# High and low f16 halves of the FFN's middle tiles: one 128x256 instruction a tile, or one of 128x512 for two tiles

## The reference, cut to what matters

```python
x = x + 0.5 * ffn(layernorm(x))          # first FFN
x = x + ssm(layernorm(x))                # state space layer, 16 states, a scan over 2048 tokens
x = x + 0.5 * ffn(layernorm(x))          # second FFN

def ffn(x):                              # x: 2048 tokens x 512
    x1 = x @ quantize(w1).T              # 512 -> 1408, weights -1, 0, 1
    x2 = x @ quantize(w2).T
    return (sigmoid(x1) * x2) @ quantize(w3).T   # 1408 -> 512
```

## Time and profile before

| what | value |
|---|---|
| median of 3 runs | 788.9 us (787.84 to 790.49) |
| span of the profiled execution | 788.1 us |
| mean granted TensorE clock | 0.942 |
| TensorE matmul busy | 644.3 us (82%), 4852 instructions |
| VectorE busy | 662.6 us (84%), 1053 instructions |
| POOL busy | 604.7 us (77%), 479 instructions |
| ScalarE busy | 530.6 us (67%), 1137 instructions |

### The profile page before, as it was taken

The page is one execution under the profiler, slowest core; times in us unless marked ns, Lnnn a source line. Parts: engine busy times, 40 slices in busy tenths (PEclk is TensorE's granted clock), DMA queues, the critical chain, the costliest instruction groups (busy, mean ns, idle before and its releaser), DMA issues.

```text
span 788.1 us, 13737 instructions
## 1 busy us (share of the span) xinstructions
PE 644.3 (82%) x4852; PEld 525.4 (67%) x4852; DVE 662.6 (84%) x1053; ACT 530.6 (67%) x1137; POOL 604.7 (77%) x479
## 2 busy tenths in 40 slices
PE   4697785579889988998899889988899887357878
PEld 3576663267668776886688767876787766245767
DVE  3872799689998999899989999899889987899721
ACT  5776665667686777766795779576867784556431
POOL 0081898589898998899889899799889978689512
PEclk9999998679999999999999999999999999578989
DMA  9500579668875897498668776788758875876000
GB/s 360 165 1 3 165 164 199 168 141 177 187 180 129 180 208 184 103 204 194 151 139 204 164 166 167 173 168 195 179 135 172 184 175 124 186 170 127 27 1 27
DMA packets 42437, 121.06 MB, mean 154 GB/s; under 512 B 5888, under 2 KB 14848, under 8 KB 42368
## 3 DMA queue, kind: packets, MB, share of 16 engines
q0 software_dynamic: 18864, 68.69, 45.9%
q1 hardware_dynamic: 23504, 51.49, 20.1%
HBM read 47.03 MB, written 4.46 MB: 65 GB/s over the span
## 4 chain that ended last, share of the span: by engine, by line
DVE 32%; PE 32%; issue 13%; ACT 13%; POOL 7%; DMA 2%; DVEq 1%; ACTq 0%; POOLq 0%
PE work L402 23%; DVE states L911 19%; PE stat L402 7%; DVE shared L922 7%; POOL hid_lo L1088 4%; ACT decay L727 3%; POOL shared L1104 2%; DMA shared<-shared 2%; DVE hid L881 2%; ACT L656 1%; PE decay L402 1%; ACT dt L715 1%; ACT q L745 1%; ACT L715 1%; ACT L659 1%
## 5 line engine op out<-in xcount | busy, mean ns | idle before, releaser
L402 PE MATMUL work<-x_hi,q 128*128 128x256 f16 x1408 | 328.0, 281 | 47.5 <-DVE hid L881 20.4
L1104 POOL TENSOR_TENSOR shared<-u,b_row 128x1024 f32<-128x1024 f32 x127 | 345.0, 2735 | 0.5
L402 PE MATMUL work<-x_lo,q 128*128 128x256 f16 x1408 | 326.9, 281 | 0.0
L911 DVE TENSOR_TENSOR_SCAN states<-decay,last_state,shared 128x256 f32<-128x256 f32 x448 | 303.7, 738 | 10.0 <-ACT decay L727 2.4
L727 ACT ACTIVATE decay<-dt,a_neg 128x256 f32<-128x256 f32 x512 | 220.2, 466 | 98.3 <-DVE states L911 97.5
L402 PEld LDWEIGHTS work<-x_hi,q 128*128 128x128 f16 x1408 | 142.3, 101 | 83.0 <-DVE hid L881 32.7
L1088 POOL TENSOR_TENSOR hid_lo<-hid,hid_hi 128x256 f16<-128x256 f32 x176 | 139.9, 1015 | 73.3 <-ACT hid_hi L690 73.1
L402 PE MATMUL work<-hid_hi,q 128*128 128x256 f16 x693 | 155.0, 274 | 14.8 <-POOL hid_lo L1088 7.8
L1117 POOL DMA_DIRECT2D shared<-shared x124 | 133.5, 1077 | 36.9 <-DVE shared L922 21.7
L922 DVE TENSOR_TENSOR shared<-states,c_row 128x1024 f32<-128x1024 f32 x128 | 155.5, 1215 | 5.8 <-issue 0.2
L402 PEld LDWEIGHTS work<-x_lo,q 128*128 128x128 f16 x1408 | 142.0, 101 | 21.8 <-issue 1.4
(11 more groups left out here) (102 smaller groups left out, 569.5 us busy)
## 6 DMA issues: line engine op xcount, KB each, us to landing
shared<-shared POOLq DMA_DIRECT2D x131, 512.0 KB, 6.2
b_row<-bc_dram SPq DMA_DIRECT2D x32, 512.0 KB, 5.1
c_row<-bc_dram SPq DMA_DIRECT2D x32, 512.0 KB, 5.2
x_in<-xT SPq DMA_DIRECT2D x8, 512.0 KB, 6.2
outT<-shared SPq DMA_DIRECT2D x7, 512.0 KB, 3.2
shared<-w1T SPq DMA_DIRECT2D x4, 704.0 KB, 7.3
shared<-w2T SPq DMA_DIRECT2D x4, 704.0 KB, 11.8
shared<-w3T SPq DMA_DIRECT2D x3, 768.0 KB, 13.5
```

The lines of the kernel that those rows point to most:

```text
L402: return nc.tensor.matmul(out, lhsT, rhs, start=start, stop=stop)
L911: nc.vector.tensor_tensor_scan(out=states[:, k, :], data0=decay[pair][:, k % 2, :], data1=dbx[:, g % DBX_RING, k, :], initial=state, op0=A ...
L1104: nc.gpsimd.tensor_tensor(dbx[:, g % DBX_RING, :, :], u[:, par, :, :], bcast(b_row[:, group % 2, n % ROWS, :]), ALU.mult).then_inc(dbx_don ...
```

## The change

ScalarE's hidden_hi and POOL's hidden_lo do nothing at the places of tiles 0, 2, 4, 6 and 8. At the places of tiles 1, 3, 5, 7 and 9 they make two tiles, (0, 1), (2, 3) and so on, with one instruction of 128x512, and add 2 to hi_done or lo_done. Tile 10 is made alone as before. The ring's two slots of a pair lie side by side in both kinds of pass. The wait for the down product of the pass before moves from tile 0's place to tile 1's. Nothing else is changed: the tables, VectorE's hidden, and TensorE's waits are the same.

```diff
             def hidden_hi(f, which, h):
-                unit = KH * f + h
-                act.wait_ge(hid_done, unit + 1)
-                if h == 0 and not (isinstance(f, int) and f == 0):
+                if h % 2 == 0 and h < KH - 1:
+                    return
+                lo, n = (h - 1, 2) if h % 2 else (h, 1)
+                act.wait_ge(hid_done, KH * f + h + 1)
+                if lo == 0 and not (isinstance(f, int) and f == 0):
                     act.wait_ge(down_done, 2 * f)
-                nc.scalar.activation(hid_hi[:, h, :], hid[:, hid_slot(which, h), :], ACT.Copy).then_inc(hi_done, 1)
+                at = hid_slot(which, lo)
+                nc.scalar.activation(hid_hi[:, lo:lo + n, :], hid[:, at:at + n, :], ACT.Copy).then_inc(hi_done, n)
...
             def hidden_lo(f, which, h):
-                unit = KH * f + h
-                pool.wait_ge(hi_done, unit + 1)
-                nc.gpsimd.tensor_tensor(hid_lo[:, h, :], hid[:, hid_slot(which, h), :], hid_hi[:, h, :], ALU.subtract).then_inc(lo_done, 1)
+                if h % 2 == 0 and h < KH - 1:
+                    return
+                lo, n = (h - 1, 2) if h % 2 else (h, 1)
+                pool.wait_ge(hi_done, KH * f + h + 1)
+                at = hid_slot(which, lo)
+                nc.gpsimd.tensor_tensor(hid_lo[:, lo:lo + n, :], hid[:, at:at + n, :], hid_hi[:, lo:lo + n, :],
+                                        ALU.subtract).then_inc(lo_done, n)
```

## The result

| what | before | after |
|---|---|---|
| median of 16 runs each, us | 790.36 (787.58 to 793.79) | 794.69 (793.57 to 797.37) |
| ratio of the times | | 1.0057, 95% interval 1.0043 to 1.0072 |
| span of the profiled execution, us | 788.1 | 792.4 |
| mean granted TensorE clock | 0.942 | 0.939 |

The changed kernel is slower by 0.57%, more than the 0.3% that a measurement can tell. The 16 runs of the kernel before that were made beside it lie 1.5 us above the three that the prediction started from, so its 793.2 us is 1.5 us under the median of after; its span, 792.4 us, is the measured one.

The account below looks back on a forecast made before the run. No engine alone bounds the kernel; POOL's low halves feed TensorE's down product, for which VectorE waits. Terms 2.7 - 0.1 + 0.9 + 0.8 = +4.3 us on 788.9 gave 793.2 us, range 789.7 to 796.3.

Parts of the forecast that it names:

- A pair on POOL: One 512-column low half on POOL takes 1.14 us; other estimates were 1.07, 1.27 and 1.53.
- Steady chunks: Second pass, chunks 1 to 5: TensorE's down product waits for tile 7 too, losing 0.54 us a chunk, +2.7 us in all.
- The residual's wait: VectorE's wait for TensorE at a steady chunk's second residual grows from 1.40 to about 1.9 us.
- ScalarE's relief: In the second pass it brings VectorE's tile 10 forward 0.1 to 0.3 us, worth nothing while VectorE waits for TensorE.
- POOL's row: In a steady chunk POOL's run of low halves ends 0.1 us later than before, counted from its DMA issue.
- Within 0.1 us of POOL's need: In a steady chunk ScalarE's high half of tiles 8 and 9 is done near 488.4, about when POOL needs it.
- Chunk 6: VectorE may stall 1 us and TensorE run 0.4 us later, covered by the 4.11 us wait: nothing, +1 us if uncovered.
- Last chunk: Steps 12 to 15: longer low halves delay TensorE's down product by 0.9 us without slack (0.5 to 1.2).
- First pass of all: Pairs run when quantising doesn't, so TensorE's tile 10 comes 0.8 us later (0.3 to 1.4).
- no change: Rival: slack the profile doesn't show absorbs the half-microsecond steps, 790.7 us; chance 0.24.
- dearer pairs: Rival: loss in the same place, with a POOL pair at 1.27 to 1.53 us, 796.2 to 800 us; chance 0.10.
- faster by POOL's relief: Rival: low halves on the chain shrink 10%, -3.2 us, 785.7 us, needing pairs of 0.90 us at most; chance 0.10.

Follow-up runs that it names:

- Run 1: Kernel after with high halves on ScalarE one tile at a time at their old places, pairs on POOL only: ratio 1.0034, span 792.4 us.
- run 4: Kernel before, nothing paired, with TensorE's second-pass down product waiting for eight tiles instead of seven: ratio 1.0022, span 792.5 us.
- run 6: The change's pairs only in the second FFN passes of the steady chunks, single instructions elsewhere: ratio 1.0041, span 793.3 us.
- run 3: Kernel after with TensorE's down product starting at six tiles instead of seven, waiting one by one from tile 6: ratio 1.0030, span 790.9 us.
- run 11: Kernel after, unchanged, profiled a second time: span 794.4 us.
- run 7: The change's pairs only in the very first pass and the last chunk's second pass, single instructions elsewhere: ratio 1.0021, span 789.3 us.
- run 5: The change's pairs only in the first FFN's passes except the very first, single instructions elsewhere: ratio 1.0010, span 789.5 us.
- run 9: Kernel before, no pairs, with tile 3's low half one place earlier on POOL, ahead of the DMA issue: ratio 0.9968, median 789.38 us.
- run 10: Kernel before, unchanged, profiled a second time: span 788.7 us.

## Why the prediction was right

It was right in sign, in size (ratio 1.0057 against 793.2 / 788.9 = 1.0055) and in the place. By its own steps:

- **A pair on POOL**: 1.14 us forecast, 1.137 measured. Taking it from the same operation at 1024 columns was the right choice: half of that, 1.07, the two single halves, 1.27, and the fold's 1.53 were all off.
- **Steady chunks**: +0.54 each forecast, +0.53 by the pitch. The down product is 0.67 us later behind the variance (0.7 forecast), and tile 10 no longer holds it. Run 1 shows that it is POOL's part, run 4 that the later gate alone is 0.31 of it, run 6 that it is these passes. The Trainium skill's Perfetto Trace Analysis, Optimizing Scalar/DVE Operations, was cited for two rules, which it gives for ScalarE and VectorE and which were applied to POOL here; the one on breaking instructions up where they cause bubbles elsewhere is what the trace bears out (TensorE's new wait of 0.41 us), though POOL's busy time fell by 14.8 us.
- **The residual's wait** was forecast at about 1.9 and is 2.16. The text had the reason, that ScalarE's relief ends in the same wait, and did not add it: tile 10's 0.25 us went there.
- **POOL's row** should have ended 0.1 us later; from the DMA issue's end it is 5.41 us (487.90 to 493.31) against 5.07, 0.34 later, by the 0.21 us that (8, 9) waits for ScalarE. "Within 0.1 us of POOL's need" was twice that. It cost nothing here, since tile 10's matmul stood at 493.64; in run 3 it took back part of the gain.
- **Chunk 6** was put at nothing and measured +0.36. The stall of VectorE for a ring slot came as described, 1.17 us at 658.22. It was hidden: VectorE waits at the residual behind it until TensorE is done, before and after (4.11 and 3.95 us). What was not hidden is TensorE's later run. The prediction counted the wait of 4.11 us as cover for it, but it is a wait for TensorE, so that the end of the down product sets it and a later end comes through. The 0.36 us that are left of the later start are that growth; the chunk's pitch is 84.46 or 84.47 in after and runs 6 and 11, and 84.10 and 84.11 in before and run 7.
- **Last chunk**: +0.9 forecast. TensorE's offset grows from 3.83 to 4.66, +0.83.
- **First pass of all**: +0.8 forecast, +0.54 measured. With chunk 6 this is the term that was mis-sized. The prediction kept pairs and quantising strictly apart and let each hold the other back. POOL and VectorE in time:

```profile
51.02 2.26 POOL L1094 TENSOR_TENSOR hid_lo<-hid,hid_hi 128x512 f16<-128x512 f32 x1 [0.37 <-ACT hid_hi L693]
53.46 3.08 POOL L1094 TENSOR_TENSOR hid_lo<-hid,hid_hi 128x512 f16<-128x512 f32 x2 [0.18 <-ACT hid_hi L693]
```

```profile
53.07 1.83 DVE L964 SCALAR_TENSOR_TENSOR q<-shared,thr,q 128x1536 f16<-128x1536 f32 x1
```

(6, 7) ends at 53.28, as forecast (53.2). But the last quantising ends at 54.90, against 52.70 + 2.14 = 54.84 before: it was not held back by 0.2 to 0.3 us. POOL ends at 56.54, not at 56.8. The pair still takes 2.26 us here against 1.137 alone, which agrees with the two engines taking turns; no run separates them. The Trainium skill's SBUF — State Buffer, SBUF: two separate sides, has the loser block for a whole instruction; the slow pair agrees, and the quantising shows that a pair twice as long need not block it for longer.

The terms as measured are 5 x 0.53 + 0.36 + 0.83 + 0.54 = 4.4 us. The waits for means and decays add 0.28 in the steady chunks, and from the last chunk's down product to the end 0.32 is taken back (4.66 to 4.34), which makes the 4.34. So the sum of 4.3 was exact partly by luck: chunk 6 was too low by 0.36 and the first pass too high by 0.26, and the other two terms nearly cancel and differ from one profile to the next. In the second profile of each kernel the spans are 788.7 and 794.4.

The rivals: "no change" fell, since no slack lay behind the residual's wait; "dearer pairs" fell with 1.137; "faster by POOL's relief" fell too, with 1.137 against the 0.90 us that it needed.

## What to carry to other kernels

Joining two instructions of a producer saves its fixed part (here 0.13 us of POOL a pair) and doubles the step in which its consumer is fed; before joining, ask which tile the consumer's first wait stands at and when the pair with it ends. Where a wait ends the chain, look for an idle gap of the producer ahead of it and move one tile in: one place in a table made this kernel faster, where eighty joined pairs made it slower. Compare chunk pitches between two like residuals rather than whole times when a step is half a microsecond: where no other wait lay between them, two profiles of one kernel agreed to 0.02 us (83.13 and 83.15) and 0.05 us (83.01 and 82.96), while their spans differed by 0.6 and 1.3 us.

## What was not expected of the hardware

- The same program has two courses through a chunk, with and without a wait of some 1.2 us for the decay on ScalarE; the pitch of the kernel after is 83.66 or 85.44 us, with single halves in the second passes 83.12 or 85.00 (run 5), and they change between executions and between chunks of one.
- The mean of a layer norm takes 8 matmuls, 2.0 us at the full granted clock. Where VectorE waits for it, they run mostly at the lower of the two clock levels, 1.2 GHz, and take up to 3.43 us (201.02 in the trace of before, at a granted clock of 0.56, and 3.33 at 368.17, at 0.58, against 1.99 at 285.05). TensorE stands idle for 2.2 to 2.3 us ahead of these matmuls in either case, so the gap alone does not tell the slow ones. In the first profile of before the pitches that end at 414.58 and 582.31 and hold such a wait have a mean granted clock of 0.98, the two without 1.00.
- The same clock step moves the second-pass down product of chunk 6. Behind a gap of 1.6 to 2.7 us it runs at 1.00 in ten profiles and at 0.74, up to the first residual, in four (runs 1, 4, 9 and 10), which costs 1.4 us, and the kernel before has it both ways.
- In the last chunk the 104 matmuls take 13.94 us after and 12.95 before, and the 176 of the tail 20.85 and 21.86. The same work takes one microsecond more in one and as much less in the other: over the 104 the mean granted clock is 0.82 after and 0.89 before, over the 176 it is 0.93 and 0.88. The loss of one is made up by the other, and the end does not show it.
